# Two DRAM read-backs of a two-layer transformer kernel, split by token block between SyncE's and GpSimd's queues

## The chip, the cores and the metric

One core of one Trainium2 chip runs the whole kernel. The metric is the device time of one execution in microseconds (us); lower is better. The kernel before takes 1522.68 us, the median of 3 runs (1517.53 to 1522.79).

The core's engines are TensorE (PE, with its weight loads shown as PEld), VectorE (DVE), ScalarE (ACT), GpSimd (POOL) and SyncE (SP). SP issues nearly all DMA transfers; the transfers themselves run on 16 DMA engines that the core has.

## What is computed

For each of 8 independent sequences of 256 tokens with 128 channels the reference does four things, each on a layer norm of x, each added to x:

```python
x = x + _L0_xattn_ref(_layernorm(x), ctx, ...)   # 16 heads of 8: causal self attention plus cross attention
x = x + _L0_ffn_ref(_layernorm(x), ...)          # 8 experts, top 2 of a router
x = x + _L1_xattn_ref(_layernorm(x), ctx, ...)   # cross attention, one head
x = x + _L1_ffn_ref(_layernorm(x), ...)          # mixture-of-values attention, below
```

The change lies in the last of them:

```python
q = einsum('btc,hdc->bhtd', x, Wq);  k = einsum('btc,hdc->bhtd', x, Wk)   # 16 heads of 64
w, sel = top_k(einsum('btc,hec->bthe', x, Ws), 2)                         # per token and head: 2 of 8 value experts
mix_v = sigmoid(w) at the chosen experts, 0 elsewhere                     # (t, head, expert)
proj_v = einsum('btc,edc->bted', x, Wv)                                   # (t, expert, 64)
v = einsum('bthe,bted->bhtd', mix_v, proj_v)                              # the mixed values
attn = softmax(q*scale @ k^T) @ v                                         # the attended values, (t, head, 64)
mask_o = top 2 of einsum('btc,hec->bthe', x, Wd)                          # 2 of 8 output experts
out = einsum('bthe,bthd,efd->btf', mask_o, attn, Wo)
```

## The kernel before

All work is float32 (some products in its replicated form), one launch, weights held in the core's memory for the whole run. A sequence is split into `NT = 2` token blocks of 128 tokens (index `t`). The work of a sequence is cut into steps: `STEPS_A` are the first three sublayers, `STEPS_B` the fourth. `merged(LAG)` lays the B steps of sequence q beside the A steps of sequence q+1 by a table of weights (`HOLD`), and every engine runs its own part of each step in that one order. So the PE stream holds, in turn, pieces of two sequences. Only the B steps of the last sequence have no partner. The change leaves this table and the order of the steps alone.

The B steps that matter, with the semaphores that join them:

- `b_mix` (PE L925, ACT L1092): for 8 tokens at a time a block-diagonal matrix `bd` of mixing weights is multiplied with the value projections. The product, the mixed values, comes out with the partitions numbered by (token within a group of 8, head). Attention wants partitions numbered by token. So SP writes each block to DRAM (`v_d`, L546, semaphore `b_vd`), and reads it back in the other order into `vb` (L553, `b_vr`). Between the writes and the reads SP issues 8 reads of the output selection into `bd` (L549).
- `b_score`: scores and exponentials into `pb`.
- `b_attend(hg)`, four times: PE L942 multiplies `pb` with `vb` for 4 heads and both query blocks. The first one waits for `b_vr`. DVE divides (L1358, L1359) into `at`, and SP writes these 4 heads of `at` to DRAM (`at_d`, L557, `b_ad`).
- `b_weigh`: after the fourth write has landed, SP reads the attended values back in four transfers of 256 KB (L565): half 0 of token block 0, half 0 of block 1, half 1 of block 0, half 1 of block 1. They raise `b_ar0` (both blocks of half 0) and `b_ar1` (both blocks of half 1). Here the order goes from tokens to (token within 8, head). The destination `atr` is a view of `at`.
- `b_gather(half)`: PE L956, 16 products for each block, waits for `b_ar0`, then for half 1 for `b_ar1`. ACT L1097 copies the result, and `b_out` (PE L967, DVE L1367) ends the sequence.

POOL does little: for the A steps it masks exponentials (L1129), for the B steps it clears `bd` twice, once at `b_gates` (L1114, waits for the previous sequence's `b_z`, which the gather raises) and once at `b_mix(1)` (L1119, waits for `b_mm`).

Transfers of mixed values are 512 KB each (128 partitions x 16 heads x 64 floats), so 2,048 contiguous pieces of 256 bytes. Transfers of attended values are 256 KB, so 1,024 pieces of 256 bytes.

Of the kernel before, what the change touches and what calls it, by code (L numbers as in the profile page):

```python
# [34 lines left out]
def transformer_program(nc, a, out):  # L35
# [5 lines left out]
    NT = T // P  # L41
# [4 lines left out]
    HB, DH, _ = a["L1_ffn_Wq"].shape  # L46
# [6 lines left out]
    with ctx:  # L53
# [96 lines left out]
        vb = sb("vb", [P, NT, HB, DH + 1])  # L150
# [7 lines left out]
        T8, TG = 8, P // 8  # L158
        pvr = pvs[:, :, :].rearrange("p t n -> p (t n)").rearrange("p (g d) -> p g d", d=DH)
        zT = pvs[:, :, :].rearrange("p t n -> p (t n)").rearrange("p (e n) -> p e n", e=E)  # L160
        atr = atf.rearrange("p (n d) -> p n d", d=DH)
# [3 lines left out]
        def dram(name, shape):  # L165
# [5 lines left out]
        v_d = dram("v_d", [NT, TG, T8, HB, DH])  # L171
        at_d = dram("at_d", [NT, TG, T8, HB, DH])
# [35 lines left out]
            b_mx=16, b_ct=1, b_cc=1, b_st=16, b_ex=16, b_mw=1, b_pd=16, b_pr=32, b_bz=2, b_md=32, b_dm=256, b_do=128,  # L208
            b_mm=4, b_ve=4, b_vd=32, b_vr=32, b_pv=8, b_at=8, b_ad=64, b_ar0=32, b_ar1=32, b_z=2, b_zc=2, b_ro=2, b_xo=2,
            a_out=16)  # L210
# [279 lines left out]
        def sequences(steps):  # L490
# [3 lines left out]
            def upto(name, n):  # L494

                return PER_SEQ[name] * now[0] + n

            with nc.Block(no_gpsimd_drain=True) as block:

                @block.sync  # L500
                def _(sp):
# [39 lines left out]
                    def b_mix(half):  # L541
                        if half != 1:
                            return
                        for t in range(NT):
                            sp.wait_ge(S["b_ve"], upto("b_ve", 3 + t))
                            sp.dma_start(v_d[t].rearrange("g s h d -> (s h) g d"), vb[:, t, :, 0:DH]).then_inc(S["b_vd"], 16)  # L546
                        sp.wait_ge(S["b_bz"], upto("b_bz", 2))
                        for i in range(T8):
                            sp.dma_start(bd_o[HB * i:HB * i + HB, :, i, :],  # L549
                                         sel_d[:, i].rearrange("n h e -> h n e")).then_inc(S["b_do"], 16)  # L550
                        sp.wait_ge(S["b_vd"], upto("b_vd", 32))
                        for t in range(NT):
                            sp.dma_start(vb[:, t, :, 0:DH], v_d[t].rearrange("g s h d -> (g s) h d")).then_inc(S["b_vr"], 16)  # L553

# [5 lines left out]
                    def b_weigh(_):  # L560
                        sp.wait_ge(S["b_ad"], upto("b_ad", 64))
                        for half in range(2):
                            for t in range(NT):
                                n = TG * t + 8 * half
                                sp.dma_start(atr[:, n:n + 8, :],  # L565
                                             at_d[t, 8 * half:8 * half + 8].rearrange("g s h d -> (s h) g d"))\
                                    .then_inc(S["b_ar1" if half else "b_ar0"], 16)

# [14 lines left out]
                def _(pe):  # L583
# [346 lines left out]
                    def b_attend(hg):  # L930

                        pe.wait_ge(S["b_ex"], upto("b_ex", 4 * hg + 4))
                        if hg == 0:
                            pe.wait_ge(S["b_vr"], upto("b_vr", 16 * NT))
                            pe.wait_ge(S["b_ve"], upto("b_ve", 2 * NT))
# [11 lines left out]
                    def b_gather(half):  # L947

                        if half == 0:
                            pe.wait_ge(S["b_ex"], upto("b_ex", HB))  # L950
                            pe.wait_ge(S["b_do"], upto("b_do", 16 * T8))
                        pe.wait_ge(S["b_ar1" if half else "b_ar0"], upto("b_ar0", 16 * NT))
                        for i in range(8):
# [156 lines left out]
                def _(pool):  # L1110
# [5 lines left out]
                    def b_mix(half):  # L1116
                        if half == 1:
                            pool.wait_ge(S["b_mm"], upto("b_mm", 2 * NT))
                            nc.gpsimd.memset(bd[:, :], 0.0).then_inc(S["b_bz"], 1)  # L1119

                    def a_score(n):
# [9 lines left out]

                    own = dict(b_gates=b_gates, b_mix=b_mix, a_score=a_score)
                    for name, i, q in steps:
# [274 lines left out]
```

## Time and profile before

| what | value |
|---|---|
| median of 3 runs | 1522.68 us |
| profiled execution, its own time | 1523.34 us |
| profiled execution, span of the instructions | 1521.6 us |
| PE busy / DVE busy / ACT busy / POOL busy | 79% / 48% / 32% / 5% of the span |
| share of PE in the chain that ended last | 70% |
| DMA queue of SP: packets, MB, share of 16 engines | 195318, 51.30 MB, 15.9% |
| mixed values read back, `vb<-v_d` | 16 transfers, 512 KB each |
| attended values read back, `at<-at_d` | 32 transfers, 256 KB each |

The span and the execution's own time lie 1.7 us apart, and the median of the runs lies 0.66 us under the profiled execution. Times in the profile are counted from the start of the span. Busy shares are averages over eight sequences and over stages that have different limits, so what the change touches has to be read in the few microseconds around each transfer.

### The profile page before, as it was taken

The page shows a single profiled execution, that of the slowest core. Times are in us where ns is not written, and L with a number is a line of the kernel's source. Part 1 is how long each engine was busy: PE and PEld are TensorE (multiplying, and loading weights), DVE is VectorE, ACT ScalarE, POOL GpSimd, SP SyncE. Part 2 cuts the span into 40 slices and gives each one's busy share as a digit, 9 for nine tenths or more (in the row PEclk, how much of TensorE's full clock was granted, in tenths as well). Part 3 has the DMA queues.
Part 4 walks back from the last instruction along what each step waited for, and adds up shares of the span by engine and source line. Part 5 has one row for each costly group of instructions (what it writes and reads, how often), then busy time and mean ns, then how long its engine had stood idle before and what let it go on. Part 6 is the DMA issues. An engine that isn't in the chain of part 4 may idle for free.

```text
span 1521.6 us, 21331 instructions
## 1 busy us (share of the span) xinstructions
PE 1203.9 (79%) x8530; PEld 933.1 (61%) x8530; DVE 723.7 (48%) x1958; ACT 490.0 (32%) x1003; POOL 79.4 (5%) x134
## 2 busy tenths in 40 slices
PE   2777778898689878898689878888779878896566
PEld 2544655696557655686558655676548655785466
DVE  2633367525672367525762368435671468322600
ACT  0222334343244324343234324333335314331111
POOL 0001000000010000000010001000010001000000
PEclk9755967698769887798769888798769887887655
DMA  6000001030303021030203021031103011022132
GB/s 177 8 0 4 1 0 29 16 67 14 67 13 57 21 46 28 17 67 22 60 13 61 17 46 36 9 74 41 33 17 60 14 46 39 18 57 46 39 66 52
DMA packets 197498, 56.85 MB, mean 37 GB/s; under 512 B 173029, under 2 KB 193303, under 8 KB 197399
## 3 DMA queue, kind: packets, MB, share of 16 engines
q1 hardware_dynamic: 195318, 51.30, 15.9%
q10 hardware_dynamic: 2080, 4.19, 0.9%
q8 instruction: 67, 1.10, 0.3%
q14 instruction: 33, 0.26, 0.1%
HBM read 31.36 MB, written 24.12 MB: 36 GB/s over the span
## 4 chain that ended last, share of the span: by engine, by line
PE 70%; DVE 13%; ACT 5%; DMA 4%; issue 4%; SPq 1%; ACTq 0%; DVEq 0%
PE bank L766 9%; PE bank L942 9%; PE bank L792 8%; PE bank L692 6%; PE bank L869 5%; PE bank L618 4%; PE bank L904 4%; PE bank L707 3%; DMA at<-at_d 2%; PE bank L925 2%; ACT pa L1012 2%; DVE negmax L1179 2%; PE bank L653 2%; PE bank L883 2%; PE bank L586 2%
## 5 line engine op out<-in xcount | busy, mean ns | idle before, releaser
L1012 ACT ACTIVATE pa<-bank 128x512 f32<-128x512 f32 x224 | 123.4, 595 | 172.5 <-PE bank L707 95.5
L1179 DVE TENSOR_REDUCE negmax<-bank 128x2 f32<-128x512 f32 (+1 forms) x224 | 138.9, 682 | 69.1 <-PE bank L653 42.6
L766 PE MATMUL bank<-xnT_a,w 128*128 128x256 f32 x512 | 144.9, 436 | 0.1
L942 PE MATMUL bank<-vb,pb 128*128 128x65 f32 x1024 | 133.1, 294 | 11.3 <-issue 11.3
L942 PEld LDWEIGHTS bank<-vb,pb 128*128 128x128 f32 x1024 | 129.6, 209 | 16.1 <-issue 14.6
L1259 DVE SCALAR_TENSOR_TENSOR x_a<-bank,wr,x_a 128x128 f32<-128x128 f32 x128 | 38.9, 345 | 207.7 <-PE bank L792 207.7
L1029 ACT ACTIVATE pa<-bank,b_c 128x256 f32<-128x256 f32 x256 | 107.5, 471 | 60.5 <-PE bank L766 59.2
L1087 ACT ACTIVATE pb<-bank 128x512 f32<-128x512 f32 x128 | 69.5, 594 | 177.2 <-PE bank L908 176.8
L792 PEld LDWEIGHTS bank<-w,pa 128*128 128x128 f32 x1024 | 123.7, 192 | 2.9
L792 PE MATMUL bank<-w,pa 128*128 128x128 f32 x1024 | 124.9, 275 | 0.0
L766 PEld LDWEIGHTS bank<-xnT_a,w 128*128 128x128 f32 x512 | 108.4, 221 | 21.3 <-issue 3.5
L692 PE MATMUL bank<-pa,va 128*32 128x256 f32 (+1 forms) x1024 | 96.2, 525 | 10.1 <-ACT pa L1012 9.5
L1331 DVE TENSOR_REDUCE negc<-bank 128x2 f32<-128x512 f32 x128 | 81.1, 684 | 17.8 <-PE bank L883 17.6
L1129 POOL TENSOR_SCALAR_AFFINE_SELECT pa<-pa 128x256 f32<-128x256 f32 (+1 forms) x96 | 47.8, 507 | 566.4 <-ACT pa L1012 565.1
L869 PE MATMUL bank<-xnT_b,wqk_t 128*128 128x256 f32 x256 | 76.6, 446 | 0.0
L707 PE MATMUL bank<-qs,ks 32*128 32x256 f32 x256 | 55.8, 462 | 25.9 <-DVE qs L1191 16.9
L586 PE MATMUL bank<-ident,xn_a 128*128 128x128 f32 x64 | 17.9, 373 | 72.8 <-DVE xn_a L389 61.0
L1358 DVE RECIPROCAL recB<-bank 128x4 f32<-128x4 f32 x64 | 11.6, 181 | 131.4 <-PE bank L942 131.1
L998 ACT ACTIVATE hi_part<-bank,lo_bias,lo_c 128x256 fp32r<-128x256 f32 x128 | 61.5, 566 | 21.0 <-PE bank L618 20.8
L692 PEld LDWEIGHTS bank<-pa,va 128*32 128x32 f32 x1024 | 39.3, 150 | 46.0 <-issue 30.2
L707 PEld LDWEIGHTS bank<-qs,ks 32*128 32x128 f32 x256 | 34.6, 269 | 51.8 <-ACT pa L1012 22.5
L1097 ACT COPY pvs<-bank 128x512 f32<-128x512 f32 x16 | 16.8, 1048 | 145.4 <-PE bank L956 145.4
(231 smaller groups left out, 1851.1 us busy)
## 6 DMA issues: line engine op xcount, KB each, us to landing
v_d<-vb SPq DMA_DIRECT2D x16, 512.0 KB, 5.0
vb<-v_d SPq DMA_DIRECT2D x16, 512.0 KB, 5.9
at_d<-at SPq DMA_DIRECT2D x32, 256.0 KB, 2.1
at<-at_d SPq DMA_DIRECT2D x32, 256.0 KB, 4.3
pv_d<-pvs SPq DMA_DIRECT2D x8, 512.0 KB, 2.8
pvs<-pv_d SPq DMA_DIRECT2D x16, 256.0 KB, 4.2
w<-in_L_ffn_W_dram ACTq DMA_DIRECT2D x1, 2048.0 KB, 9.9
bd<-mix_d SPq DMA_DIRECT2D x128, 8.0 KB
```

The costliest lines, as they stand in the source:

```text
L692: mm = pe.matmul(dst, va[:, sc, kt, h * DV:h * DV + 32], rhs, start=(kt == 0), stop=(sc == SELF or kt == 1), skip_group_check=True)
L707: mm = pe.matmul(BA[i][:, kt * T:(kt + 1) * T], ks[strips[i], CROSS, k, kt * P:(kt + 1) * P], qs[strips[i], CROSS, k, :], start=True, stop ...
L766: mm = pe.matmul(BA[u % 2][:, c * T:(c + 1) * T], w1[:, e, f:f + P], xnT_a[:, :], start=True, stop=True)
L792: mm = pe.matmul(BA[2 + e % 2][:, t * P:(t + 1) * P], hT[:, (2 * e + f // 2) % 4, f % 2, t * P:(t + 1) * P], w2[:, e, f, :], start=(f == 0 ...
L869: mm = pe.matmul(BB[(u + 2) % 4][:, c * T:(c + 1) * T], wqk_t[:, u // 4, 2 * (u % 4) + c, :], xnT_b[:, :], start=True, stop=True)
L942: mm = pe.matmul(BB[2 + qt][:, i * (DH + 1):(i + 1) * (DH + 1)], pb[:, h % NPB, kt * T + qt * P:kt * T + (qt + 1) * P], vb[:, kt, h, :], s ...
L998: nc.scalar.activation(hi_part[:, n % 4, :].bitcast(F32R), BA[u % 4][:, c * T:(c + 1) * T], ACT.Identity, bias=lo_bias[:, k:k + 1], scale= ...
L1012: nc.scalar.activation(pa[:, e % NPA, :], BA[e % 2][:, :], ACT.Exp, scale=SC0).then_inc(S["a_ex"], 1)
L1029: ins = nc.scalar.activation(hT[:, u % 4, c, :], BA[u % 2][:, c * T:(c + 1) * T], ACT.Relu, bias=b1_c[:, k:k + 1])
L1087: nc.scalar.activation(pb[:, h % NPB, :], BB[h % 2][:, :], ACT.Exp, scale=SC1).then_inc(S["b_ex"], 1)
L1179: nc.vector.tensor_reduce(negmax[:, i:i + ng], BA[j][:, :].rearrange("p (g k) -> p g k", g=ng), AX, ALU.max, negate=True).then_inc(S["a_mx ...
L1331: nc.vector.tensor_reduce(negc[:, qt, c:c + 3:2], BB[(n + 2) % 4][:, :].rearrange("p (h k) -> p h k", h=2), AX, ALU.max, negate=True).then ...
```

## The change

Of each pair of reads that go by token block, the one of block 0 stays on SP's queue and the one of block 1 goes to POOL's queue. Each gets a semaphore of its own (`b_vr1`, `b_ap0`, `b_ap1`), and PE waits for both where it waited for one that counted both.

```diff
-                        for t in range(NT):
-                            sp.dma_start(vb[:, t, :, 0:DH], v_d[t].rearrange("g s h d -> (g s) h d")).then_inc(S["b_vr"], 16)
+                        sp.dma_start(vb[:, 0, :, 0:DH], v_d[0].rearrange("g s h d -> (g s) h d")).then_inc(S["b_vr"], 16)
...
                         for half in range(2):
-                            for t in range(NT):
-                                n = TG * t + 8 * half
-                                sp.dma_start(atr[:, n:n + 8, :],
-                                             at_d[t, 8 * half:8 * half + 8].rearrange("g s h d -> (s h) g d"))\
-                                    .then_inc(S["b_ar1" if half else "b_ar0"], 16)
+                            n = 8 * half
+                            sp.dma_start(atr[:, n:n + 8, :],
+                                         at_d[0, 8 * half:8 * half + 8].rearrange("g s h d -> (s h) g d"))\
+                                .then_inc(S["b_ar1" if half else "b_ar0"], 16)
...
                         if hg == 0:
-                            pe.wait_ge(S["b_vr"], upto("b_vr", 16 * NT))
+                            pe.wait_ge(S["b_vr"], upto("b_vr", 16))
+                            pe.wait_ge(S["b_vr1"], upto("b_vr1", 16))
...
-                        pe.wait_ge(S["b_ar1" if half else "b_ar0"], upto("b_ar0", 16 * NT))
+                        pe.wait_ge(S["b_ar1" if half else "b_ar0"], upto("b_ar0", 16))
+                        pe.wait_ge(S["b_ap1" if half else "b_ap0"], upto("b_ap0", 16))
...
                         if half == 1:
                             pool.wait_ge(S["b_mm"], upto("b_mm", 2 * NT))
                             nc.gpsimd.memset(bd[:, :], 0.0).then_inc(S["b_bz"], 1)
+                            pool.wait_ge(S["b_vd"], upto("b_vd", 32))
+                            pool.dma_start(vb[:, 1, :, 0:DH], v_d[1].rearrange("g s h d -> (g s) h d")).then_inc(S["b_vr1"], 16)
+
+                    def b_weigh(_):
+                        pool.wait_ge(S["b_ad"], upto("b_ad", 64))
+                        for half in range(2):
+                            n = TG + 8 * half
+                            pool.dma_start(atr[:, n:n + 8, :],
+                                           at_d[1, 8 * half:8 * half + 8].rearrange("g s h d -> (s h) g d"))\
+                                .then_inc(S["b_ap1" if half else "b_ap0"], 16)
```

What this does to SP's stream, at the B steps of one sequence from the write of the mixed values to the output (line numbers of the changed kernel behind the +; `bd<-sel_d` are the 8 reads of the output selection):

```order
 L546 DMA v_d<-vb 128x16x64 x2
 L549 DMA bd<-sel_d 16x32x8 x8
-L553 DMA vb<-v_d 128x16x64 x2
-L557 DMA at_d<-at 128x2x256 x4
-L565 DMA at<-at_d 128x8x64 x4
-L571 DMA out_dram<-x_b 128x2x128
+L552 DMA vb<-v_d 128x16x64
+L556 DMA at_d<-at 128x2x256 x4
+L563 DMA at<-at_d 128x8x64 x2
+L569 DMA out_dram<-x_b 128x2x128
```

One read of `vb` and two reads of `at` are gone from SP; nothing else in its order moves. What it does to POOL's stream, between the second clearing of `bd` in one sequence and the masks of the next A steps:

```order
+L1139 AFFINE_SELECT pa<-pa 128x512 x2
 L1119 MEMSET bd 128x2048
+L1121 DMA vb<-v_d 128x16x64
+L1127 DMA at<-at_d 128x8x64 x2
 L1114 MEMSET bd 128x2048
-L1129 AFFINE_SELECT pa<-pa 128x2x128 x4
```

The three reads stand between the two clearings; no mask of the A steps stands between them.

## Rows read from the trace of the kernel before

**Rows 1.** The page: busy time by engine, share of span, instructions.

```profile
PE 1203.9 (79%) x8530; PEld 933.1 (61%) x8530; DVE 723.7 (48%) x1958; ACT 490.0 (32%) x1003; POOL 79.4 (5%) x134
```

**Rows 2.** The page: the chain that ended last, shares of the span by engine.

```profile
PE 70%; DVE 13%; ACT 5%; DMA 4%; issue 4%; SPq 1%; ACTq 0%; DVEq 0%
```

**Rows 3.** The waits, whole span: total us, times, longest.

```profile
POOL bd L1114 <- PE bank L956: 527.3, 7, 77.5
...
PE bank L956 <- DMA at<-at_d: 38.7, 14, 7.5
```

**Rows 4.** Timeline, second sequence's return of attended values: start, length, engine, [idle <-releaser].

```profile
548.79 0.36 SPq L557 DMA_DIRECT2D at_d<-at  x1
...
550.92 2.88 SPq L565 DMA_DIRECT2D at<-at_d  x4
...
551.63 2.48 DVE L1179 TENSOR_REDUCE negmax<-bank 128x2 f32<-128x512 f32 x4 [0.48 <-PE bank L653]
...
555.53 3.86 PE L956 MATMUL bank<-bd,at 128*64 128x64 f32 x64 [3.82 <-DMA at<-at_d]
```

**Rows 5.** DMA in forty slices of 0.25 us, from 550 to 560 us.

```profile
DMA  9700000044999999999999999993000000000000
GB/s 348 262 4 0 0 0 0 15 96 99 233 288 291 286 288 239 201 216 215 225 223 223 223 217 221 184 216 59 0 0 0 0 0 0 0 0 0 0 0 0
```

**Rows 6.** The chain of waits there: start, length, what.

```profile
552.86 4.75 DMA at<-at_d
...
557.65 1.77 PE bank L956 x32
```

**Rows 7.** By line: L565 (attended values) issue and landing.

```profile
L565 SPq DMA_DIRECT2D at<-at_d x32: 359/675/1132, 382.0 to 1508.0; - x32
...
DMA to landing us min/median/max: 3.2/4.3/4.8
```

**Rows 8.** By line: L553 (mixed values) issue and landing.

```profile
L553 SPq DMA_DIRECT2D vb<-v_d x16: 554/918/1972, 320.6 to 1458.2; - x16
...
DMA to landing us min/median/max: 4.7/5.9/8.4
```

**Rows 9.** DMA in forty slices of 0.5 us, last sequence, 1448 to 1468 us.

```profile
GB/s 0 0 0 0 178 221 215 191 223 220 227 223 223 190 24 43 19 40 24 33 29 30 145 223 262 287 217 198 251 246 219 56 1 0 0 0 0 0 0 0
```

**Rows 10.** Timeline of SP's issues and PE, last sequence, mixed values.

```profile
1449.11 1.91 SPq L546 DMA_DIRECT2D v_d<-vb  x2
...
1451.05 6.54 SPq L549 DMA_DIRECT2D bd<-sel_d  x8
...
1457.64 2.16 SPq L553 DMA_DIRECT2D vb<-v_d  x2
...
1464.77 7.06 PE L942 MATMUL bank<-vb,pb 128*128 128x65 f32 x32 [11.26 <-issue]
```

**Rows 11.** DMA in forty slices of 0.5 us, first sequence, 308 to 328 us.

```profile
GB/s 0 0 0 33 0 0 0 0 0 0 174 217 217 193 221 219 226 223 225 194 26 41 21 35 29 32 32 26 153 188 261 282 170 181 246 260 245 136 0 0
```

**Rows 12.** Timeline there: the reads, and PE's first use.

```profile
320.64 2.07 SPq L553 DMA_DIRECT2D vb<-v_d  x2
...
331.76 3.69 PE L942 MATMUL bank<-vb,pb 128*128 128x65 f32 x32
```

**Rows 13.** POOL by line and form: busy us, mean ns, idle before.

```profile
L1129 POOL TENSOR_SCALAR_AFFINE_SELECT pa<-pa 128x256 f32<-128x256 f32 x64 | 28.3, 442 | 551.8 <-ACT pa L1012 550.5
...
L1119 POOL MEMSET bd<- 128x2048 f32 x8 | 14.4, 1805 | 276.6 <-PE bank L925 276.6
...
L267 POOL MEMSET negc<- 128x256 f32 x1 | 0.3, 305 | 0.0
```

**Rows 14.** DVE in the last us before gathers: length, busy, PEclk, DMA.

```profile
551.00:556.00 5.00, 2.63 (x5) 0.62 0.96 179
...
1384.00:1388.70 4.70, 0.00 (x0) 0.61 0.90 169
```

More of the change, by code:

```diff
@@ L208, in transformer_program @@
             b_mx=16, b_ct=1, b_cc=1, b_st=16, b_ex=16, b_mw=1, b_pd=16, b_pr=32, b_bz=2, b_md=32, b_dm=256, b_do=128,
-            b_mm=4, b_ve=4, b_vd=32, b_vr=32, b_pv=8, b_at=8, b_ad=64, b_ar0=32, b_ar1=32, b_z=2, b_zc=2, b_ro=2, b_xo=2,
+            b_mm=4, b_ve=4, b_vd=32, b_vr=16, b_vr1=16, b_pv=8, b_at=8, b_ad=64, b_ar0=16, b_ar1=16, b_ap0=16, b_ap1=16, b_z=2, b_zc=2, b_ro=2, b_xo=2,
             a_out=16)
@@ L1130, in a_score @@
                                                     pattern=[[0, blocks], [1, P]], channel_multiplier=-1).then_inc(S["a_sl"], 1)
-                    own = dict(b_gates=b_gates, b_mix=b_mix, a_score=a_score)
+                    own = dict(b_gates=b_gates, b_mix=b_mix, b_weigh=b_weigh, a_score=a_score)
                     for name, i, q in steps:
```

## The prediction, made before the changed kernel was run

> **What bounds the kernel now.** I read the busy times first. PE works 79% of the span, no other engine above 48%, POOL 5% [rows 1], and 70% of the chain that ended last is PE's [rows 2]. So an edit counts only where PE waits for it. Next the waits by who was waited for. PE waits 38.7 us in all for the read-back of attended values, 14 waits, the longest 7.5 us [rows 3]. That is the only wait of PE for a transfer that the change touches and that repeats in every sequence. POOL's own wait for the gather, 527.3 us, costs nothing, since POOL has no other work then [rows 3].
>
> Then I looked at one such place in order of time, the second sequence's [rows 4]. The last write of `at` is issued at 548.79, the four reads from 550.92 on, and PE starts the gather at 555.53 after 3.82 us of idleness. PE takes its instructions in order, and the A steps behind the gather cannot pass it. The other seven sequences look the same (3.7 to 3.9 us of idleness in five of them, 7.4 and 7.5 us in the last two, where less A work fills the time before).
>
> What is short in these 4.6 us? SP takes 2.88 us to issue four reads [rows 4], which looks like a queue that could be split. But the DMA row says otherwise. In slices of 0.25 us the 16 engines reach their highest digit at 552.5 and hold it up to 556.75, moving 200 to 290 GB/s [rows 5]. All four reads (1.05 MB in 4,096 pieces of 256 bytes) go through in one saturated stretch. The fourth read is issued at 552.86 and lands 4.75 us later, and the second gather starts 0.04 us after that [rows 6]. The issues run ahead of the engines. From the end of the data near 556.75 to PE's start at 557.65 another 0.9 us pass, which is the time a transfer needs to report.
>
> The other place is the read-back of mixed values. In the first sequence, which stands for seven, the reads are issued at 320.64 and PE needs them at 331.76, when it comes from other work without an idle stretch [rows 12]. The data ends near 326.9 [rows 11], so they are in 4 us early. Only in the last sequence, with no A steps beside it, does PE stand idle for them: 11.26 us, up to 1464.77 [rows 10].
>
> **Part by part: what goes.** SP loses one 512 KB issue (median 0.92 us, [rows 8]) and two of 256 KB (median 0.68 us, [rows 7]) a sequence. If the engines were not full, the second read of half 0 could start 0.4 us earlier. I count this at zero. The cover is the saturated stretch: bytes and pieces stay what they were, and the same 16 engines move them. If that cover were absent, the gain would be that of the third rival below.
>
> The engines being full agrees with a rule of the Trainium skill (DMA: Bandwidth & Descriptors, "Issuing engines are not separate DMA queues"), which speaks against this change: transfers started from SyncE and from GpSimd run on the same engines, and a second issuer saves only issue time. The trace agrees, with the highest digit for 4.25 us [rows 5]. By the rule alone the sum would be the third rival's gain at most.
>
> **What moves past what.** POOL's three new reads stand between its two clearings of `bd`. The first read waits for `b_vd`, the next for `b_ad`. Behind them is the clearing L1114, which waits for the gather anyway, and the gather comes after all of these reads. So no work of POOL is held up, and no mask of the A steps stands behind a read. PE's second wait at each place costs nothing beyond what it waits for. SP, relieved, reaches its next work early, and that again waits for DVE or PE.
>
> **What comes: the cost of a read on POOL.** The trace of before has no DMA from POOL, so I bound the time in which POOL can set up one 256 KB read of 1,024 pieces. Below: what SP needs, 0.36 us [rows 7]. Above: a piece has a source and a destination entry, so 2,048 entries. POOL's clearing writes 2,048 columns in 1.81 us, 0.88 ns a column [rows 13]. If each entry is written as four words one by one, that is 2,048 x 4 x 0.88 ns = 7.2 us. Between the two I take one step for each entry, 1.81 us, made dearer because an entry is computed and not only stored: a mask of 128x256 takes 442 ns where a clearing of 128x256 takes 305 ns, 1.45 times as long [rows 13]. So 1.81 x 1.45 = 2.6 us for a 256 KB read, 5.2 us for a 512 KB read. The engines cannot finish before the last entry is there.
>
> *Attended values, 8 times.* A read lands 3.2 us after SP starts the issue at best, so 2.84 us after the 0.36 us of issue [rows 7]. Half 0 of block 1: 550.92 + 2.6 + 2.84 = 556.36, so the first gather starts near 556.4 instead of 555.53. Half 1 of block 1 comes behind it on POOL: 550.92 + 5.2 + 2.84 = 558.96, so the second gather starts at 559.0 instead of 557.65 [rows 6]. That is 1.35 us, and all that follows (ACT's copy, the output, PE's A steps) moves with it. 8 x 1.35 = 10.8 us.
>
> *Mixed values, last sequence.* The writes of `v_d` fall off at 1455.0 [rows 9], and 0.9 us later POOL may start: 1455.9, where SP starts at 1457.64 because eight issues stand before it [rows 10]. POOL needs 5.2 us, and a 512 KB read lands at best 4.7 - 0.55 = 4.15 us after its issue [rows 8]: 1465.25 against PE's start at 1464.77. That is 0.5 us later.
>
> *Mixed values, seven other sequences.* The same from 318.0 + 0.9 [rows 11]: 318.9 + 5.2 + 4.15 = 328.25, while PE comes at 331.76 [rows 12]. Hidden, with 3.5 us to spare; the cover is PE's expert and score work. It would be gone if POOL needed over 8.7 us for 512 KB.
>
> **The sum.** 10.8 + 0.5 = 11.3 us on the profiled execution's own 1523.34 us (span 1521.6) gives 1534.6 us. That execution lies 0.66 us above the median of the runs shown, so I forecast 1534 us, 0.7% slower. What a measurement of this kernel can tell from no change is about 0.5%, 7.6 us.
>
> The Trainium skill gives a first byte about 0.4 us later for GpSimd's transfers than for SyncE's (DMA: Bandwidth & Descriptors, "Latency and other measured facts"), and says that many descriptors can be emitted before they cost (same page, "Anatomy of one DMA — SWDGE (gpsimd) path"). No row of this trace bears on either. As an estimate by these alone the change would cost 8 x 0.4 = 3 us, 1526 us, inside the next case.
>
> **Rivals.**
>
> *POOL is quick enough, and the full engines tie the two orders (no change).* At one plain step for each entry, 1.81 us a read, half 0 lands at 555.57 and half 1 with the end of the saturated stretch, as now. What is left is sharing: SP's half 1 now competes with POOL's half 0, up to 0.5 us for the first gather (a quarter of a stretch of 2 us), 8 x 0.5 = 4 us, less 1.0 us in the last sequence (1455.9 + 3.6 + 4.15 = 1463.7). 1522 to 1526 us. For it: rows 5, and the cheapness of POOL's plain instructions. Against it: POOL would have to build entries as fast as it clears memory.
>
> *POOL is much dearer (slower by far).* At 4.5 us a read half 1 lands at 562.8, 5.15 us late, 41 us over eight; the last sequence's mixed values come 4.3 us late, and the seven others just lose their cover (0.3 us each). 1570 us. At the upper bound of 7.2 us it is 84 + 10 + 7 x 5.7 = 134 us, 1657 us. For it: an entry has several words. Against it: nothing in the trace.
>
> *The issue was the limit (faster).* If two queues feed the engines better, POOL's first read goes out at 550.92 together with SP's, 0.4 us ahead of now, and the data runs at the 288 GB/s of the first part of the stretch instead of 220 [rows 5]: 1.05 MB in 3.65 us, 0.9 us sooner. The second gather must follow the first, so the gain is 0.4 us, 3.2 us over eight, plus 1.7 us in the last sequence (1457.64 - 1455.9). 1518 us. It decides only if POOL sets up a read in under 0.8 us or so. Even then it stays inside 0.5%.
>
> *VectorE keeps POOL from writing its entries (slower).* DVE is busy 2.63 of the 5 us before the gather in six of the eight sequences, and not at all in the last two (one window of each kind stands in [rows 14]). If POOL stood still in that time, 6 x 2.6 = 16 us come on top, 1550 us. Against it: these DVE rows are reductions of a PSUM bank [rows 4]. The Trainium skill (SBUF — State Buffer, "SBUF: two separate sides") has such a lock for VectorE's fast modes, as in a float32 copy within SBUF, and none stands in this stretch. It would show as a longer delay in six sequences than in the last two.
>
> **How the numbers follow.** Forecast (POOL 2.2 to 3.5 us a read, 1528 to 1553 us): 0.40. No change: 0.30. Much dearer: 0.15. Issue the limit: 0.08. VectorE's lock: 0.07. The upper end reaches into the dearer case up to 4.5 us a read, the lower one to the third rival's time: 1518 to 1570 us. Slower by over 0.5% (above 1530.3): most of the forecast (0.36), the dearer case and the lock, 0.58. Within 0.5%: 0.36. Faster by more needs 0.95 us in each sequence, more than any row offers: 0.06.
>
> **What would show it.** On POOL three rows of DMA issue in each sequence, near 2.6 us for `at` and 5.2 us for `vb`, tell the price directly. PE's wait before the first gather should grow from 3.8 to some 4.7 us, and a second wait of about 0.5 us should appear before half 1, released by POOL's reads and not by SP's. The DMA row there should show the highest digit for SP's 512 KB and lower digits after it, ending near 558 instead of 556.75. The mixed values of seven sequences should show no wait. I am wrong if the second gather starts within 0.3 us of its old distance from the last write, or if PE waits for `vb` in the middle sequences.

## The result, and the profile after

The changed kernel takes 1554.11 us, the median of 4 runs (1549.61 to 1556.85), beside 1521.9 us for the kernel before (4 runs). The ratio is 1.0215, with a 95% interval of 1.0183 to 1.0246. The forecast was 1534 us with a range of 1518 to 1570: the direction and the range hold, the size does not. It was 12 us in the forecast and is 32 us. In the tables below a ratio leaves out the slow runs, those over 1.5% above the fastest of their kernel, while a median is of all runs.

From here on gather 1 and gather 2 are the products of half 0 and of half 1 of the attended values. The page of the changed kernel, the row that answers to [rows 1], and its two DMA queues (packets, MB, share of 16 engines; q0 is POOL's):

```profile
PE 1231.2 (79%) x8530; PEld 954.5 (62%) x8530; DVE 724.3 (47%) x1958; ACT 490.6 (32%) x1003; POOL 102.8 (7%) x158
...
q1 hardware_dynamic: 162166, 42.91, 13.2%
q0 software_dynamic: 2432, 8.39, 2.4%
```

PE is busy 27.3 us longer than in [rows 1], with the same 8530 matmuls. The span grew by 30.1 us (1521.6 to 1551.7). So most of the loss is in products that take longer, and no wait is in it. The waits themselves, beside [rows 3]:

```profile
POOL at L1127 <- DMA at_d<-at: 472.5, 8, 62.5
...
PE bank L956 <- DMA at<-at_d: 46.1, 9, 8.6
```

PE's wait for the attended values grew from 38.7 to 46.1 us, 7.4 us in all, a quarter of the loss. (27.3 and 7.4 are more than 30.1, since other idle time of PE shrank.) The place itself, second sequence, beside [rows 4]:

```profile
550.80 0.36 SPq L556 DMA_DIRECT2D at_d<-at  x1
...
552.94 0.99 SPq L563 DMA_DIRECT2D at<-at_d  x2
553.21 1.75 POOL L1127 DMA_DIRECT2D at<-at_d  x2 [62.53 <-DMA at_d<-at]
...
558.61 3.68 PE L956 MATMUL bank<-bd,at 128*64 128x64 f32 x64 [4.89 <-DMA at<-at_d]
```

From the issue of the last write to gather 1 it was 6.74 us (548.79 to 555.53) and is 7.81 us (550.80 to 558.61). Over all eight sequences gather 1 comes 7.05, 6.74, 6.62, 6.68, 6.78, 6.79, 6.80 and 6.66 us after that issue before, and 7.34, 7.81, 7.93, 7.77, 7.95, 7.95, 7.67 and 7.90 us after the change, 1.0 us later in the mean. Gather 2 comes 0.68 us later in the mean (8.90 to 9.58), because in the changed kernel its data is there when gather 1 ends (one stretch of 64 products, no idleness between).

POOL's two lines, issue in ns (min/median/max) and landing, answering to [rows 7] and [rows 8]:

```profile
L1127 POOL DMA_DIRECT2D at<-at_d x16: 882/882/891, 380.7 to 1536.1; - x16
...
DMA to landing us min/median/max: 4.8/5.4/6.0
```

```profile
L1121 POOL DMA_DIRECT2D vb<-v_d x8: 1149/1167/1283, 317.3 to 1484.7; - x8
...
DMA to landing us min/median/max: 6.6/6.8/7.4
```

The instruction of a 256 KB read takes 0.88 us on POOL, that of a 512 KB read 1.17 us. The forecast had 2.6 and 5.2. Yet the landing, 5.4 us after the issue, is what the forecast had (2.6 + 2.84 = 5.44). The DMA row there in slices of 0.25 us, from 552 to 562 us, and the queues' packets, beside [rows 5]:

```profile
GB/s 352 275 8 0 0 0 0 11 143 141 232 280 271 261 293 291 286 307 241 178 191 214 264 246 213 98 33 0 0 0 66 0 0 0 0 0 0 0 0 0
...
q1 hardware_dynamic: 2251, 0.68, 29.0%
q0 software_dynamic: 160, 0.52, 24.3%
```

SP's queue moves its half in 2,080 packets, 2,048 of 256 bytes and 32 of 4 bytes (the row counts the tail of the write before it too), POOL's in 160, 128 of 4,096 bytes and 32 of 4. I added up the packets of each queue in the trace in slices of 0.5 us:

```
us       SP queue KB   POOL queue KB
553.5          2              0
554.0         69              0
554.5        125              0
555.0        130              0
555.5        126             16
556.0         40            104
556.5          6             96
557.0         10             88
557.5          0            124
558.0          0             76
558.5          0              8
```

POOL's first packet starts at 555.75, 2.54 us after its issue begins (1.8 us in the first sequence, 2.2 to 2.6 us in the others; SP's: 553.96, 1.02 us after). By then SP has moved most of both its reads. From then on POOL's large packets take most of what the engines move, and SP's last 16 KB take from 556.5 to 557.5. The last byte is through 5.9 us after SP's first issue, against 6.1 us before (550.92 to 557.02). So the same bytes take the same time; what got late is the quarter that gather 1 needs from POOL.

The mixed values, last sequence, beside [rows 10]:

```profile
1478.09 1.71 SPq L546 DMA_DIRECT2D v_d<-vb  x2
...
1484.65 1.15 POOL L1121 DMA_DIRECT2D vb<-v_d  x1 [5.30 <-DMA v_d<-vb]
...
1493.74 6.63 PE L941 MATMUL bank<-vb,pb 128*128 128x65 f32 x30 [11.24 <-DMA vb<-v_d]
```

From the first write of `v_d` to the first use it is 15.65 us, and was 15.66 us (1449.11 to 1464.77). Nothing changed there, and in the other sequences PE does not wait for them.

Where are the other 24 us? The next rows cut the run from one gather 1 to the next. Columns: length, busy time of PE, PEld, DVE, ACT and POOL (instructions; POOL's three reads, 2.9 us, count in its own), granted clock of PE, DMA share, GB/s. Two such periods of the kernel before:

```profile
555.50:726.30 170.80, 142.58 (x1057) 110.13 (x1058) 88.70 (x238) 61.10 (x125) 9.63 (x14) 0.80 0.17 37
897.00:1064.10 167.10, 138.67 (x1056) 108.00 (x1056) 88.57 (x238) 60.81 (x125) 9.63 (x14) 0.83 0.18 38
```

and one after:

```profile
558.60:732.90 174.30, 146.84 (x1058) 114.46 (x1058) 88.84 (x238) 61.01 (x125) 12.55 (x17) 0.77 0.17 36
```

The same work takes 170.8, 167.1 and 174.3 us, and PE's busy time moves with it: 142.6, 138.7 and 146.8 us. DVE, ACT and POOL's masks do not change. Full periods of the kernel before are 168.9, 170.8, 170.7, 167.1 and 170.9 us; those of the changed kernel 173.0, 174.3, 174.0, 174.2 and 174.1 us. The first 8 us after gather 1, before:

```profile
555.50:563.50 8.00, 7.12 (x122) 6.32 (x123) 3.36 (x8) 2.10 (x2) 1.80 (x1) 0.78 0.22 35
897.00:905.00 8.00, 7.11 (x123) 6.23 (x124) 3.40 (x9) 2.10 (x2) 1.81 (x1) 0.79 0.22 36
```

and after:

```profile
558.60:566.60 8.00, 7.58 (x102) 7.18 (x104) 2.48 (x4) 2.10 (x2) 1.80 (x1) 0.50 0.01 2
```

Before, the granted clock is back at 2.4 GHz within these 8 us (0.78 and 0.79 in the mean). After, it is at 0.50 through all of them, that is 1.2 GHz. It is so in six of the eight sequences after the change, in one before. The output products, which stand right there, show it (before, then after; mean ns and total):

```profile
L967 PE MATMUL bank<-wo_t,pvs 64*128 64x128 f32 x256 | 18.0, 295 | 6.2 <-ACT pvs L1097 6.2
```

```profile
L967 PE MATMUL bank<-wo_t,pvs 64*128 64x128 f32 x256 | 26.8, 390 | 4.7 <-ACT pvs L1097 4.7
```

They took 18.0 us and take 26.8 us, 8.8 us more for the same 256 products. Over the whole run PE stands at the lower level for 669 us before and for 748 us after (mean granted clock 0.780 and 0.759).

There is a second place. Before, the periods that begin at 726.3 and 897.0 differ (170.7 and 167.1 us) though their first 8 us are alike (0.79 and 0.79). What differs lies 27 to 38 us behind gather 1. The same stretch in those two periods, and in the period from 732.9 after the change:

```profile
753.60:763.80 10.20, 9.96 (x31) 6.40 (x32) 6.30 (x10) 5.97 (x11) 0.00 (x0) 0.50 0.01 2
924.40:934.60 10.20, 9.62 (x72) 5.99 (x72) 8.73 (x15) 7.47 (x14) 0.81 (x2) 1.00 0.00 0
762.40:772.60 10.20, 10.20 (x31) 6.61 (x32) 6.01 (x9) 6.10 (x11) 0.00 (x0) 0.50 0.01 2
```

In 10.2 us PE gets through 31 products at 0.50 and 72, not all of one size, at 1.00. This stretch has a slow part in three of the first six periods before and in all six after. So a period of 167.1 us is slow in neither place, one of 170.7 us in the second alone, one of 174.2 us in both.

All this was read off the traces alone, so whether the later gather causes it was still to be shown.

### The profile page after: what moved, and what is told of

It is laid out like the page before. It is cut to its first block, busy times and chain, and to the rows that moved or that the text cites. A ratio compares the mean times of both kernels' runs of the same rounds, so it can differ in the third digit from the quotient of the medians.

```text
span 1551.7 us, 21355 instructions
## 1 busy us (share of the span) xinstructions
PE 1231.2 (79%) x8530; PEld 954.5 (62%) x8530; DVE 724.3 (47%) x1958; ACT 490.6 (32%) x1003; POOL 102.8 (7%) x158
## 3 DMA queue, kind: packets, MB, share of 16 engines
q10 hardware_dynamic: 2080, 4.19, 0.9%
## 4 chain that ended last, share of the span: by engine, by line
PE 70%; DVE 13%; ACT 5%; DMA 5%; issue 3%; SPq 1%; ACTq 0%; DVEq 0%
PE bank L764 9%; PE bank L941 8%; PE bank L790 7%; PE bank L690 6%; PE bank L867 5%; PE bank L616 4%; PE bank L902 4%; PE bank L705 3%; DMA at<-at_d 3%; PE bank L923 2%; DVE negmax L1189 2%; ACT pa L1012 2%; PE bank L956 2%; PE bank L967 2%; PE bank L651 2%
## 5 line engine op out<-in xcount | busy, mean ns | idle before, releaser
L867 PE MATMUL bank<-xnT_b,wqk_t 128*128 128x256 f32 x256 | 85.3, 485 | 0.0
L867 PEld LDWEIGHTS bank<-xnT_b,wqk_t 128*128 128x128 f32 x256 | 58.1, 242 | 15.0 <-issue 6.4
```

The costliest lines, as they stand in the source:

```text
L867: mm = pe.matmul(BB[(u + 2) % 4][:, c * T:(c + 1) * T], wqk_t[:, u // 4, 2 * (u % 4) + c, :], xnT_b[:, :], start=True, stop=True)
```

## The experiments

Each run is given as the ratio to the kernel before on the same chip, with its 95% interval.

| run | median us | ratio | interval |
|---|---|---|---|
| mixed values alone on POOL | 1527.8 | 1.0011 | 0.9990 to 1.0032 |
| attended values alone on POOL | 1553.5 | 1.0187 | 1.0165 to 1.0208 |
| three small writes, no POOL | 1551.7 | 1.0175 | 1.0153 to 1.0198 |
| changed kernel, 34 products of filling | 1544.1 | 1.0101 | 1.0065 to 1.0138 |
| split by half instead of block | 1554.9 | 1.0171 | 1.0146 to 1.0196 |
| ACT's queue in POOL's place | 1527.2 | 1.0004 | 0.9973 to 1.0035 |
| before, 14 products of filling | 1533.9 | 1.0039 | 1.0012 to 1.0065 |
| changed, 17 products of filling | 1532.6 | 1.0036 | 1.0015 to 1.0058 |
| one small write | 1517.2 | 0.9963 | 0.9941 to 0.9984 |
| six small writes | 1542.9 | 1.0131 | 1.0106 to 1.0156 |
| before, 10 products of filling | 1530.5 | 1.0052 | 1.0034 to 1.0069 |
| changed, 13 products of filling | 1535.0 | 1.0082 | 1.0059 to 1.0106 |
| changed, two small writes more | 1546.4 | 1.0116 | 1.0091 to 1.0141 |
| changed, five small writes more | 1559.6 | 1.0203 | 1.0179 to 1.0228 |
| two small writes | 1542.4 | 1.0072 | 1.0043 to 1.0100 |

### Which of the two splits: mixed values alone, attended values alone

The first kernel keeps of the change only `pool.dma_start(vb[:, 1, ...])`, the second only POOL's `b_weigh`.

> Only the mixed values' block 1 is read on GpSimd's queue; the attended values are read by SyncE as before. The theory (two thirds of the loss is TensorE at its lower clock for longer after the later gather, one third the later gather itself) expects nothing here, since in the changed kernel TensorE waits for the mixed values in the last sequence alone, and there about as long as before: 1520 to 1525 us. Rival 1, GpSimd's transfers disturb the core wherever they run, expects about a third of the loss, since 8 of the 24 reads on GpSimd are left: 1530 to 1538 us.

> Only the attended values' block 1 is read on GpSimd's queue; the mixed values are read by SyncE as before. The theory expects the whole loss here: 1549 to 1556 us, the second gather about 1.2 us later in each sequence, and after each gather one stretch less at the full clock. Rival 1 (each GpSimd transfer costs wherever it runs) expects two thirds of the loss: 1541 to 1546 us.

The mixed values alone cost nothing that can be told (1.0011; 1527.8 us is just over the expected range), the attended values alone cost nearly all (1.0187 of 1.0215). The last sequence of the first kernel, where PE does wait for them:

```profile
1453.13 1.85 SPq L546 DMA_DIRECT2D v_d<-vb  x2
...
1459.98 1.16 POOL L1121 DMA_DIRECT2D vb<-v_d  x1 [5.59 <-DMA v_d<-vb]
...
1469.42 7.06 PE L942 MATMUL bank<-vb,pb 128*128 128x65 f32 x32 [11.88 <-DMA vb<-v_d]
```

From the first write of `v_d` to the first use it is 16.29 us here, 0.6 us more than before, and that once in the run. So POOL's eight reads of 512 KB cost nothing by being there. POOL's reads cost where PE waits for them in every sequence.

### A delay without POOL

```diff
                     def b_weigh(_):
                         sp.wait_ge(S["b_ad"], upto("b_ad", 64))
+                        for k in range(3):
+                            r = 3 * now[0] + k
+                            sp.dma_start(dl_d[r:r + 1, :], ident[0:1, 0:16]).then_inc(S["b_dl"], 16)
```

> Nothing is on GpSimd's queue; SyncE issues three writes of 64 bytes to a scratch tensor (about 0.38 us of issue each) before it issues the four reads of the attended values. So the reads come 1.1 to 1.3 us late by themselves. The theory (the delay and the clock that follows from it make the loss) expects a loss of the changed kernel's size, 1545 to 1558 us, with TensorE's busy time up by 20 us or more at the same number of matmuls. Rival 2, that the delay alone costs 8 x 1.2 us and the rest comes from how GpSimd's transfers get at memory, expects 1531 to 1534 us and TensorE's busy time as before.

Gather 1 came 0.8 us later than before (7.4 to 7.8 us after the last write's issue), and the kernel's ratio was 1.0175. One period and its first 8 us:

```profile
555.00:729.10 174.10, 145.56 (x1056) 112.65 (x1056) 88.73 (x238) 61.07 (x125) 9.62 (x14) 0.78 0.17 36
```

```profile
555.00:563.00 8.00, 7.40 (x97) 6.81 (x98) 2.48 (x4) 2.10 (x2) 1.80 (x1) 0.50 0.19 31
```

174.1 us, PE at half clock after the gather, PE busy 145.6 us: the changed kernel's period, with nothing on POOL. Over the whole trace PE is busy 20.3 us longer than before (1224.2 us), for the same 8530 products. This showed that a delay of gather 1 makes a loss of this size without POOL's queue, and that 0.8 us of delay can cost 27 us.

### By half, and with ACT's queue

The kernel by half has SP read half 0 of both blocks and POOL half 1 of both. The other one is the split by block, with `act.dma_start` in place of `pool.dma_start`.

> Mixed values on SyncE as before. The attended values are split by half instead of by token block: SyncE reads half 0 of both blocks, GpSimd half 1 of both. The theory, in which what counts is how late the gathers come and how long TensorE's clock then stays low, expects the first gather where it was before, and the second up to 1 us late, since GpSimd's reads land about 1 us later than SyncE's: TensorE works in between and its idle stretch is not longer. 1522 to 1540 us, well under the 1553 us of the split by block. Rival 1 (GpSimd's transfers cost wherever they are) expects 1549 to 1556 us.

> The split of the attended values by token block, with ScalarE's queue in GpSimd's place; mixed values on SyncE as before. If the delay of the first gather comes from GpSimd's own path (its issue of 0.88 us and its later landing), ScalarE's queue has none of it, and the full transfer engines leave no gain: 1518 to 1530 us. If it comes from two queues that share full engines, whoever issues, the first gather is late here too: 1540 to 1556 us.

The split by half missed its expectation: 1.0171. Second sequence, the issues and gather 1:

```profile
553.67 0.99 SPq L564 DMA_DIRECT2D at<-at_d  x2
553.94 1.78 POOL L1123 DMA_DIRECT2D at<-at_d  x2 [69.01 <-DMA at_d<-at]
...
559.35 3.68 PE L954 MATMUL bank<-bd,at 128*64 128x64 f32 x64 [4.90 <-DMA at<-at_d]
```

All that gather 1 needs was issued by SP at 553.67 to 554.66, and still it started 5.68 us after, not 4.6 us. The packets show why. POOL's begin at 556.53. In the half microsecond from 556.7 POOL's queue moves 112 KB and SP's 40 KB, and in the next two 108 and 104 KB beside 4 and 5 KB. SP's last packet ends at 558.11. So POOL's queue holds back a transfer that SP issued first. Its packets are 16 times as large; whether their size does it or something else in POOL's queue, no run separates. With ACT's queue in its place:

```profile
552.67 0.36 SPq L557 DMA_DIRECT2D at_d<-at  x1
...
554.81 0.99 SPq L564 DMA_DIRECT2D at<-at_d  x2
554.81 1.16 ACTq L1099 DMA_DIRECT2D at<-at_d  x2
...
559.69 1.97 PE L956 MATMUL bank<-bd,at 128*64 128x64 f32 x32 [4.11 <-DMA at<-at_d]
```

The packets of both queues have 256 bytes here, and neither queue is pushed aside for long: in the half microseconds from 556.7 to 559.7 SP's moves 41 to 78 KB and ACT's 29 to 91. The period of the third sequence is

```profile
727.10:894.20 167.10, 138.48 (x1056) 107.90 (x1057) 88.53 (x238) 60.75 (x125) 9.62 (x14) 0.84 0.18 37
```

as short as the shortest before, though gather 1 comes 0.3 us later in the mean over the sequences (in the second, above, 7.02 us after the last write, against 6.74). The total is no change: 1.0004, with runs from 1519 to 1543 us. But the total moves with the clock. That two issuers gain nothing on full engines is shown by the gathers of this run, which has neither POOL's late start nor its large packets: gather 1 comes 0.3 us and gather 2 0.4 us later than before, and not earlier.

### Keeping PE busy over the wait

```diff
                             pe.wait_ge(S["b_do"], upto("b_do", 16 * T8))
+                            for k in range(17):
+                                pe.matmul(BB[0][:, 0:P], ident[:, :], ident[:, :], start=True, stop=True)
```

> The changed kernel, with 34 products of the identity with itself (128x128, float32) put on TensorE ahead of the first gather's wait, into a bank that the gather overwrites; they take some 4 to 5 us that TensorE would idle. The output is unchanged. The theory expects that TensorE stays at its full clock over the wait, so the clock's part of the loss goes and more with it, since the kernel before also fell to half clock here: 1500 to 1530 us. Rival 2 (no part of the clock) expects no gain: 1550 to 1560 us.

> The changed kernel with 17 such products, about 4.8 us, instead of 34, which at 0.28 us each ran 4 us over the data's arrival. The theory expects the 8 gathers some 1.2 us later than in the kernel before filled the same way, and the clock's part gone: 1508 to 1530 us, and 8 to 16 us above the kernel before with 14 products. Without a part of the clock: 1550 to 1558 us.

> The changed kernel with 13 products instead of 17, 4.7 us, inside its 4.9 us of idleness. The first gather 7.9 us after the last write's issue, as in the changed kernel; the clock's part gone as with 17, and the 0.6 to 1.1 us of the overshoot too: 1522 to 1532 us. Without a part of the clock: 1550 to 1558 us.

> The kernel before, with 14 products of the identity with itself ahead of the first gather's wait; the output is unchanged. The run with 34 of them showed 0.28 us for each, so these take about 3.9 us, the idle time there. The theory expects that the clock is at its full level sooner after the gather than in the kernel before: 1500 to 1518 us. Without a part of the clock: 1520 to 1528 us.

> The kernel before with 10 products of the identity instead of 14. The 14 took 5.0 us at 0.36 us each and so held up the first gather by 1.1 us; 10 take 3.6 us and fit into the 3.8 us of idleness. The first gather should start where it does in the kernel before (6.7 us after the last write's issue) and run at the full clock: 1510 to 1524 us. If the clock gives nothing back, 1522 to 1530 us.

With 34 products the filling ran to 566.75 in the second sequence, some 4 us past the data, and the kernel still gained (1.0215 to 1.0101), though at 1544 us it missed the 1500 to 1530 us expected. With 17 it is 1533 us and 1.0036, by work that computes nothing. By the ratios, each taken against the kernel before beside it (1521.9 and 1527.0 us), the gain is 27 us. The run is still 3 us over its expected range and no slower than the kernel before with 14 products, where 8 to 16 us more were expected. A period of it and its first 8 us:

```profile
730.50:900.30 169.80, 145.46 (x1092) 113.30 (x1092) 88.67 (x238) 60.81 (x125) 12.55 (x17) 0.83 0.17 37
```

```profile
730.50:738.50 8.00, 6.15 (x124) 4.95 (x124) 4.86 (x18) 2.02 (x2) 1.81 (x1) 1.00 0.06 18
```

The clock stands at its full level after the gather, and over the whole trace PE is at the lower level for 663 us, not 748. This showed that most of the loss is the clock's: the delay is still there, gather 1 comes 8.6 us after the last write in the mean (7.8 without filling). 13 products gave 1535 us, also 3 us over their expected range.

The filling of the kernel before missed. 14 products came out at 1.0039, 10 at 1.0052, so both are slightly slower, where 1500 to 1518 us and 1510 to 1524 us were expected. The 14 took 5.0 us and held gather 1 up by 1.1 us. The 10 did not (6.90 us after the last write), but the periods are 170.7 us in a row, where the kernel before has 170.8 and 167.1 us mixed. Filled, before and after the change, the kernels meet near 1530 to 1535 us. The trace with 10 products shows what keeps the kernel before from gaining. The filling lifts the clock behind the gather to 1.00, but the second place, 27 us on, stays slow in the periods of 170.7 us:

```profile
753.40:763.70 10.30, 10.16 (x31) 6.59 (x32) 6.20 (x10) 6.10 (x11) 0.00 (x0) 0.50 0.00 0
```

And gather 2 still starts 8.87 us after the last write in the mean (8.90 before), since it waits for its data. Over the whole trace PE is at the lower level for 673 us, as before (669). Why the second place is slow or fast stays open.

### How the loss depends on the delay

> As the run with three small writes on SyncE ahead of the four reads of the attended values, but with one, so some 0.35 us of delay; GpSimd's queue unused. Theory, with the clock as a step and not in proportion: the run on ScalarE's queue came 0.3 us late at the first gather and lost nothing (ratio 1.0004), so this one should lose next to nothing: 1520 to 1532 us. Rival, each part of a microsecond of delay costs its share of the 27 us that 0.8 us cost: 1535 to 1540 us.

> The kernel before with two small writes ahead of the four reads. Between one write (1517 us, periods mostly 167.1 us) and three (1552 us, periods 174.1 us). By when TensorE resumes: periods of both kinds, 1520 to 1552 us, wherever the step lies; a trace in which most periods are neither near 167.1, 170.7 nor 174.1 us would speak against it.

> As before, with six small writes, so some 2 us of delay, 1.2 us more than with three. If the clock's part is a step that three writes had already passed, only the direct delay is added, 8 x 1.2 = 10 us: 1558 to 1566 us. If it grows in proportion, the loss is some 2.5 times that of three writes: 1585 to 1600 us.

The loss does not grow with the delay. One write makes the kernel faster (0.9963, below its expected range), two cost 1.0072 with runs from 1524 to 1555 us (its four longest runs are left out; the medians of all runs stand at 1.0103), three cost 1.0175, six only 1.0131. For six both expected ranges failed, 1558 us and more against 1543. Gather 1 came 0.25, 0.5, 0.8 and 1.7 us later than before (means over the eight sequences of each trace; the trace with two writes is of one of its long executions, with a span of 1552.8 us and five periods of 173.9 to 174.1 us). Two periods of the kernel with one write:

```profile
552.90:720.10 167.20, 138.54 (x1056) 107.94 (x1057) 88.61 (x238) 60.73 (x125) 9.62 (x14) 0.84 0.18 37
888.20:1061.60 173.40, 145.50 (x1056) 112.60 (x1056) 88.73 (x238) 61.06 (x125) 9.62 (x14) 0.79 0.17 35
```

and one with six, with its first 8 us and its second place:

```profile
729.00:899.60 170.60, 140.86 (x1058) 110.08 (x1058) 88.61 (x238) 60.79 (x125) 9.62 (x14) 0.81 0.17 37
729.00:737.00 8.00, 7.42 (x98) 6.82 (x100) 2.48 (x4) 2.10 (x2) 1.80 (x1) 0.50 0.18 29
756.40:766.60 10.20, 8.22 (x53) 5.28 (x53) 8.80 (x14) 7.01 (x14) 0.41 (x1) 1.00 0.13 17
```

With one write four of five full periods are 167.1 to 168.1 us, and the one where gather 1 came 7.76 us after the last write is 173.4 us. The first period aside, they are 170.5 to 171.1 us with six and 174.0 to 174.2 us with three. So without filling a period other than the first is near 167.1, 170.7 or 174.1 us and seldom far from one of them, and the delay has a hand in which. The 170.6 us with six are not those of the kernel before: the place behind the gather is slow (0.50), and the second one is fast (1.00).

If that is so, the changed kernel must gain from being delayed further. These two kernels put the small writes ahead of the fourth write of the attended values:

> The changed kernel, with two writes of 64 bytes on SyncE ahead of the fourth write of the attended values, so everything behind comes another 0.7 us later (first gather some 8.7 us after the division, where six small writes on the kernel before put it). If the clock depends on when TensorE resumes, this kernel becomes FASTER by the delay, like the six writes: 1538 to 1550 us against 1554. If it depends on how long TensorE idles, it becomes slower: 1559 to 1575 us.

> The same with five such writes, some 1.8 us later than the changed kernel. By when TensorE resumes: the period of a sequence is one of a few values some 3.4 us apart (167.1, 170.7, 174.1 us in the traces so far), so 1545 to 1565 us, no more than 10 us above the changed kernel although 14 us of delay are added. By how long TensorE idles: 1568 to 1600 us.

It does. With two writes more, all that follows starts some 0.7 us later, and the ratio falls from 1.0215 to 1.0116; the intervals (1.0183 to 1.0246 and 1.0091 to 1.0141) do not meet. (Each is against the kernel before that was measured beside it.) In its trace, whose span of 1548.7 us is at the upper end of its runs, one period of five is 171.0 us:

```profile
733.80:908.00 174.20, 144.59 (x1056) 112.12 (x1057) 88.77 (x238) 61.12 (x125) 12.55 (x17) 0.78 0.17 36
908.00:1079.00 171.00, 140.46 (x1058) 109.64 (x1058) 88.82 (x238) 60.98 (x125) 12.54 (x17) 0.82 0.17 37
```

With five writes, some 1.8 us in each of eight sequences, it is 1.0203, no more than the changed kernel. A cost that only grows with the idle time cannot do this. In its trace PE is busy for 1221.6 us, 9.6 us less than in the changed kernel. Its five full periods are 173.6 to 174.1 us, but the clock is back within the 8 us behind gather 1 (0.74 to 0.79); what the clock gives back the longer wait takes. So a period of 174 us alone does not tell which of the two was lost.

The wait and the clock together account for all twelve traces without filling. As an estimate fitted to them, a span is 1521 us, plus 0.36 us for each microsecond at the lower level above 669, plus 0.55 us for each microsecond by which the eight gathers 2 start later after the last division than before. No trace lies more than 2.5 us off. For the changed kernel that is 28 us for the clock (79 us more at the lower level) and 3 us for the wait.

## Why the prediction was right or wrong

**Right: what bounds, and where.** The engines are full during the four reads, the bytes end at the same time after the issue (5.9 and 6.1 us), and a second issuer gains nothing. ACT's queue shows it without POOL's costs: its gathers come 0.3 and 0.4 us later, and the total is 1.0004. With that the rule of the Trainium skill that the forecast weighed (DMA: Bandwidth & Descriptors, "Issuing engines are not separate DMA queues") holds here. The mixed values are hidden in seven sequences and unchanged in the last (0.5 us forecast, 0 measured in the changed kernel; 0.6 us with them alone). Nothing of POOL's own work was held up.

**Wrong in its parts, right in their sum by luck: a read on POOL.** The forecast had 2.6 us of setting up for 256 KB, in which POOL is held; the instruction takes 0.88 us, and 1.17 us for 512 KB. What it left out is that POOL's first packet starts 2.54 us after its issue begins, where SP's starts after 1.02 us. What POOL does between the end of the instruction and the first packet no row shows. Both ways POOL's first read lands some 5.4 us after its issue. Gather 1 was to come 0.87 us later and comes 1.07 us later in that sequence; POOL's first issue begins 0.27 us behind SP's (553.21 and 552.94), where the forecast had both at one time. Gather 2 was to come 1.35 us later and comes 0.68 us later in the mean, because the second read is ready so soon after the first.

**The step that failed.** "That is 1.35 us, and all that follows (...) moves with it. 8 x 1.35 = 10.8 us." The term of the waits was too large: 8 x 0.68 is 5.4 us. What follows does not only move, it runs slower. The forecast put the clock at nothing without giving a reason. PE stands at 1.2 GHz for 79 us more (669 to 748 us) and is busy 27.3 us longer for the same matmuls. I had read the clock in [rows 14], 0.62 and 0.61 ahead of the gather, and not asked what it does behind it. The row to ask for was the 8 us after the gather, 0.78 there. The whole size does not stand in that row, since the second place, 27 us on, is slow more often as well. That a wait for DMA lets TensorE fall to its low clock, and that the work behind it then starts slow, stands in the Trainium skill (TensorE: Matmul & The Clock Gate, "HAM oscillation — how this bites in real kernels"); the trace agrees, with 0.50 in the 8 us behind the changed kernel's gather. How much it costs does not follow from the wait alone: with five writes more the wait is longer and the clock there 0.75.

**The rivals.** No change: wrong. POOL much dearer: wrong, POOL sets up a read three times as fast as forecast, not slower. The issue as the limit: wrong. DVE's lock: nearest in time (1550 us) and wrong in its mechanism, since the delay of gather 1 is the same in the last two sequences (0.87 and 1.24 us) as in the six before (0.29 to 1.31). None of the rivals had the clock in it.

## What to carry to other kernels

Before a wait of an engine whose clock depends on its load is priced at its own length, read the granted clock in the stretch behind it: here 0.7 us of delay in each of eight sequences cost 3 to 5 us by itself and 25 to 28 us by the clock. A test for it is cheap: add the same delay by other means, and add more; if the time jumps or falls, the length of the wait is not what costs. Here one needless write gave 0.9963 and three gave 1.0175, so in this kernel a small tuning step can gain or lose up to 2% for no reason of its own. Filling the wait is no sure remedy: it helped the changed kernel and not the one before. Split transfers over two issuers only where the issue is what is waited for, not where the row of DMA shares is at its top.

## What the hardware showed that was not expected

- POOL's queue moves rows of 256 bytes in packets of 4,096 bytes (128 for 512 KB), SP's and ACT's in one packet a row. While both are in flight, POOL's gets most of the engines: 104 against 40 KB in half a microsecond, then 96 against 6.
- POOL's instruction takes 0.88 us for 1,024 rows and 1.17 us for 2,048, so 0.29 us for 1,024 rows more. Its first packet starts 1.8 to 2.6 us after the start of the issue, SP's 1.02 to 1.03 us after.
- The time from one sequence to the next is mostly near 167.1, 170.7 or 174.1 us. Delays of 0.25, 0.8 and 1.7 us at one place move it to the first, the third and the second of these. A place 27 us behind the wait changes its clock along with them (0.50 or 1.00), though the work there is the same.
- The fastest kernel measured is the one before with one needless write of 64 bytes in each sequence: 1517.2 us, 0.9963 (0.9941 to 0.9984). It is no version to keep, since it owes its time to where the clock happens to stand: in its own trace one full period of five is 173.4 us.
